# Attention scores from queries and keys split into a rounded part and a rest

## What is computed

```python
def _L1_xattn_ref(x, context, Wq, Wk, Wv, Wo, bo):
    HEADS, DIM_HEAD = 16, 64
    SCALE = DIM_HEAD ** (-0.5)
    q = (x @ Wq).reshape(B, N, HEADS, DIM_HEAD).transpose(0, 2, 1, 3)
    k = (context @ Wk).reshape(B, M, HEADS, DIM_HEAD).transpose(0, 2, 1, 3)
    v = (context @ Wv).reshape(B, M, HEADS, DIM_HEAD).transpose(0, 2, 1, 3)
    dots = jnp.einsum('bhnd,bhmd->bhnm', q, k) * SCALE
    attn = jax.nn.softmax(dots, axis=-1)
    out = jnp.einsum('bhnm,bhmd->bhnd', attn, v)
    out = out.transpose(0, 2, 1, 3).reshape(B, N, HEADS * DIM_HEAD)
    return out @ Wo + bo
# L2 is the same with HEADS = 8
x = x + _L1_xattn_ref(_layernorm(x, axis=-1), ctx_768, ...)
...
x = x + _L2_xattn_ref(_layernorm(x, axis=-1), ctx_768, ...)
```

## Time and profile before

| | |
|---|---|
| median of 3 runs | 1681.1 us (1678.39 to 1681.11) |
| the profiled execution | 1681.9 us |
| its span, first to last instruction | 1679.2 us |
| l1x, first to last scores matmul | 342.2 to 705.3 us |
| l2x, first to last scores matmul | 829.6 to 1026.5 us |
| busy over the whole span | PE 86%, DVE 59%, ACT 47%, POOL 36% |

### The profile page before, as it was taken

One profiled execution on the slowest core, in us unless ns is written; L12 is line 12 of the kernel. 1 busy time (PEld: TensorE's weight loads), 2 busy tenths in 40 slices (PEclk: granted clock), 3 DMA queues, 4 the chain that ended last, 5 costly groups with the idle time before them and its releaser, 6 DMA issues. The chain is left out here.

```text
span 1679.2 us, 28447 instructions
## 1 busy us (share of the span) xinstructions
PE 1436.1 (86%) x9255; PEld 1137.2 (68%) x9255; DVE 985.6 (59%) x2396; ACT 793.9 (47%) x1920; POOL 604.3 (36%) x807
## 2 busy tenths in 40 slices
PE   4698999699999999959699997884877569999995
PEld 3477888577777777735477675463544459989885
DVE  3768888855555555559666655445775624334342
ACT  2543444465555555448665654432757333333331
POOL 0137999463343443330264442000102622222222
PEclk9789999899999999989799999897888679999998
DMA  8000023319500000010000001005003821111110
GB/s 279 20 13 20 23 98 112 99 57 291 143 2 1 2 2 1 1 38 1 16 1 1 2 1 56 20 1 220 36 1 101 281 80 52 47 52 48 53 45 6
DMA packets 67340, 97.47 MB, mean 58 GB/s; under 512 B 7792, under 2 KB 56832, under 8 KB 66176
## 3 DMA queue, kind: packets, MB, share of 16 engines
q1 hardware_dynamic: 61920, 82.94, 15.8%
q0 software_dynamic: 5280, 12.74, 2.3%
HBM read 61.86 MB, written 35.63 MB: 58 GB/s over the span
## 5 line engine op out<-in xcount | busy, mean ns | idle before, releaser
L1325 POOL TENSOR_SCALAR XT<-XT,l1x_rs 128x256 f32<-128x256 f32 x256 | 117.7, 478 | 191.5 <-DVE l1x_rs L1209 191.5
L2502 PE MATMUL bank<-l3x_wd,CT 128*128 x624 | 146.4, 389 | 9.2 <-issue 8.7
L1213 DVE TENSOR_REDUCE l1x_nmax<-bank 128x2 f32<-128x512 f32 x128 | 87.4, 684 | 109.9 <-PE bank L1035 109.9
L1152 ACT ACTIVATE XT<-bank,l1x_nmax 128x256 f32<-128x256 f32 x256 | 118.8, 471 | 68.5 <-DVE l1x_nmax L1213 68.5
L2490 PEld LDWEIGHTS bank<-XT,l3x_qw 128*128 128x128 f32 x1248 | 148.0, 195 | 3.5 <-issue 0.9
L2490 PE MATMUL bank<-XT,l3x_qw 128*128 128x128 f32 x1248 | 148.4, 278 | 1.0 <-issue 0.5
L2502 PEld LDWEIGHTS bank<-l3x_wd,CT 128*128 128x128 f32 x624 | 117.8, 194 | 28.6 <-issue 13.3
L1047 PE MATMUL bank<-ident,XT 128*128 128x128 f32 x768 | 120.7, 280 | 7.5 <-DVE l2x_pt L1220 3.5
L759 DVE SCALAR_TENSOR_TENSOR X<-bank,l0f_gates,X 128x256 f32<-128x256 f32 x288 | 118.9, 473 | 0.7 <-PE bank L683 0.7
L1047 PEld LDWEIGHTS bank<-ident,XT 128*128 128x128 f32 x768 | 84.6, 140 | 41.3 <-issue 20.7
L1220 DVE COPY l1x_pt<-bank 128x512 f32<-128x512 f32 x128 | 87.8, 686 | 30.8 <-PE bank L1047 30.8
(11 more groups left out here) (526 smaller groups left out, 3887.3 us busy)
## 6 DMA issues: line engine op xcount, KB each, us to landing
slots<-blank SPq DMA_DIRECT2D x9, 1987.5 KB, 22.2
l3x_wu<-in_L_ffn_W SPq DMA_DIRECT2D x8, 1024.0 KB
l3x_wd<-in_L_ffn_W SPq DMA_DIRECT2D x8, 1024.0 KB
XT<-slots SPq DMA_DIRECT2D x39, 132.5 KB, 2.1
l0f_wu<-in_L_ffn_upT SPq DMA_DIRECT2D x18, 128.0 KB, 2.2
l0f_wd<-in_L_ffn_downT SPq DMA_DIRECT2D x18, 128.0 KB, 2.4
X<-in_x SPq DMA_DIRECT2D x1, 2048.0 KB, 8.2
l0x_later<-in_L_xattn_W_f1T SPq DMA_DIRECT2D x1, 2048.0 KB
```

Of the source, the lines that this page charges most:

```text
L1152: act.activation(pr[n % 3][:, i, q, :], sc[(2 * n + i) % 3][:, q * S:(q + 1) * S], ACT.Exp, bias=nmax[:, n % 3, i, q:q + 1], accum_out=sum ...
L1213: dve.tensor_reduce(nmax[:, n % 3, i, :], sc[(2 * n + i) % 3][:].rearrange("p (q s) -> p q s", q=QT), AX, ALU.max, negate=True).then_inc(m ...
L1325: pool.tensor_scalar(t, t, rs[:, n % 3, i, q:q + 1], 1.0, ALU.mult, ALU.mult).then_inc(norm_ok, 1)
L2502: last = pe.matmul(y_b[i % 2][:, 0:D], hT[i % 2][:, m, :], wd[:, ds(e * HT + m, 1), :].rearrange("p a n -> p (a n)"), start=m == 0, stop=m ...
```

## The change

The tile `qk` becomes two float32r tiles. ACT writes the rounded part `qk_hi` from the PSUM bank, and a new DVE operation, `low_qk`, subtracts it from the same bank into `qk_lo`. The scores become three products into the same PSUM region, hi x hi, hi x lo and lo x hi, with the two heads alternating inside each term. Three waits are added: `scores(n)` waits for `qklo_ok`, a unit that follows a qk unit in its bank waits for `qklo_ok` too, and `low_qk` waits for ACT's copy of its unit and for the earlier scores on its buffer. `low_qk` stands in DVE's queue between the maximum of head 1 and the copy of head 1. `LEAD` is 4.

```diff
@@ -902,7 +902,7 @@
         xn = [flat[:, 3072 + s * 512:3584 + s * 512].rearrange("p (t d) -> p t d", t=QT) for s in range(2)]
         xhi, xlo = ([sb(f"{n}{s}", [P, KD, S], F32R) for s in range(2)] for n in ("xhi", "xlo"))
         chi, clo = ([sb(f"{n}{s}", [P, kt, S], F32R) for s in range(2)] for n, kt in (("chi", 2), ("clo", 1)))
-        qk = [sb(f"qk{s}", [P, 2, S]) for s in range(LEAD)]
+        qk_hi, qk_lo = ([sb(f"qk{n}{s}", [P, 2, S], F32R) for s in range(LEAD)] for n in ("hi", "lo"))
         v = [sb(f"v{s}", [P, 2, CH]) for s in range(2)]
         pt = [sb(f"pt{s}", [P, 2, 2 * S]) for s in range(2)]
         ohi, olo = ([sb(f"{n}{s}", [P, 2, S], F32R) for s in range(2)] for n in ("ohi", "olo"))
@@ -910,8 +910,8 @@
 
         w_hi, wqk_lo, wv_lo, wo_lo, w_zero, bo_ok, split_done = (
             K.sem(f"{name}_{x}") for x in ("whi", "wqklo", "wvlo", "wolo", "wzero", "bo", "split"))
-        xn_ok, xlo_ok, c_hi, c_ok, unit_done, unit_read = (
-            K.sem(f"{name}_{x}") for x in ("xn", "xlo", "chi", "c", "unitdone", "unitread"))
+        xn_ok, xlo_ok, qklo_ok, c_hi, c_ok, unit_done, unit_read = (
+            K.sem(f"{name}_{x}") for x in ("xn", "xlo", "qklo", "chi", "c", "unitdone", "unitread"))
         s_done = [K.sem(f"{name}_sdone{i}") for i in range(2)]
         pv_done = [K.sem(f"{name}_pvdone{i}") for i in range(2)]
         max_done, exp_done, rs_ok, norm_ok, t_done, pt_ok = (
@@ -979,6 +979,8 @@
                         pe.wait_ge(unit_read, number[before[u]] + 1)
                         if before[u][0] == "x":
                             pe.wait_ge(xlo_ok, before[u][1] + 1)
+                        if before[u][0] == "qk":
+                            pe.wait_ge(qklo_ok, before[u][1] + 1)
                     if kind == "x":
                         pe.wait_ge(xn_ok, QT * (m + 1))
                         for k in range(KD):
@@ -1029,13 +1031,16 @@
                     pe.wait_ge(unit_read, number["qk", n] + 1)
                     if 4 * n - 2 > 0:
                         pe.wait_ge(exp_done, 4 * n - 2)
+                    pe.wait_ge(qklo_ok, n + 1)
+                    hi, lo = qk_hi[n % LEAD], qk_lo[n % LEAD]
                     for q in range(QT):
-                        for i in range(2):
-                            r = slice(i * DH, (i + 1) * DH)
-                            last = pe.matmul(sc[(2 * n + i) % 3][:, q * S:(q + 1) * S], qk[n % LEAD][r, 0, q * P:(q + 1) * P],
-                                             qk[n % LEAD][r, 1, :], start=True, stop=True)
-                            if q == QT - 1:
-                                last.then_inc(s_done[i], 1)
+                        for term, (x, y) in enumerate(((hi, hi), (hi, lo), (lo, hi))):
+                            for i in range(2):
+                                r = slice(i * DH, (i + 1) * DH)
+                                last = pe.matmul(sc[(2 * n + i) % 3][:, q * S:(q + 1) * S], x[r, 0, q * P:(q + 1) * P], y[r, 1, :],
+                                                 start=term == 0, stop=term == 2)
+                                if q == QT - 1 and term == 2:
+                                    last.then_inc(s_done[i], 1)
 
                 def turn(n, i):
                     pe.wait_ge(norm_ok, 2 * QT * n + QT * (i + 1))
@@ -1114,7 +1119,7 @@
                         if m >= LEAD:
                             for i in range(2):
                                 act.wait_ge(s_done[i], m - LEAD + 1)
-                        act.activation(qk[m % LEAD][:], t, ACT.Copy).then_inc(unit_read, 1)
+                        act.activation(qk_hi[m % LEAD][:], t, ACT.Copy).then_inc(unit_read, 1)
                     elif kind == "m":
                         act.activation(view.row[0:1, m, :], place[u][0:1, 0:P], ACT.Copy).then_inc(unit_read, 1)
                     elif kind == "s":
@@ -1204,6 +1209,14 @@
                     dve.tensor_tensor(xlo[b % 2][:], place["x", b][:].rearrange("p (a s) -> p a s", a=2), xhi[b % 2][:].bitcast(F32),
                                       ALU.subtract).then_inc(xlo_ok, 1)
 
+                def low_qk(m):
+                    dve.wait_ge(unit_read, number["qk", m] + 1)
+                    if m >= LEAD:
+                        for i in range(2):
+                            dve.wait_ge(s_done[i], m - LEAD + 1)
+                    dve.tensor_tensor(qk_lo[m % LEAD][:], place["qk", m][:].rearrange("p (a s) -> p a s", a=2), qk_hi[m % LEAD][:].bitcast(F32),
+                                      ALU.subtract).then_inc(qklo_ok, 1)
+
                 def inverse(n):
                     dve.wait_ge(exp_done, 4 * (n + 1))
                     dve.reciprocal(rs[:, n % 3, :, :], sums[:, n % 3, :, :]).then_inc(rs_ok, 1)
@@ -1276,6 +1289,8 @@
                 for k in range(2):
                     dve.wait_ge(w_hi, 4 + k + 1)
                     lo_part(raw_v, wv, k, wv_lo, rows=HALF_C if k else P)
+                low_qk(0)
+                low_qk(1)
                 for n in steps[1:]:
                     if (n - 3) % HP == 0 and 1 <= (n - 3) // HP < B:
                         add((n - 3) // HP - 1)
@@ -1290,6 +1305,8 @@
                         copy_turned(n, 0)
                     if 0 <= n + 2 < N:
                         maximum(n + 2, 1)
+                    for kind, m in first[n]:
+                        low_qk(m)
                     if view and n >= 1:
                         look(n - 1)
                     if 0 <= n < N:
```

## The result

The changed kernel takes 1685.5 us at the median against 1679.4 us for the kernel before on the same chip: ratio 1.0033, 95% interval 1.0022 to 1.0043. A repeat on another occasion gave 1.0052 (1.0035 to 1.0068), and is among the experiments. So it is slower, by a third to half of a per cent. The forecast was about 1682 us, 0.8 us more than before, with a chance of 0.35 for slower. The measured median lies inside the range of 1672 to 1698 us, but the change costs about 6 us and not 0.8.

The account below looks back on a forecast made before the run. The prediction took PE's queue to bound both stages. Shorter scores and added waits summed to -15.4 + 4.9 + 11.3 = +0.8 us, taking the profiled 1681.9 to 1682.7 us and the median to about 1682; range 1672 to 1698 us.

Parts of the forecast that it names:

- The scores: Scores of each step: six slots of 0.12 us, 0.91 us instead of 1.07, 15.4 us less over 96 steps.
- Rival 1: Scores: the slot is 0.11 us, 21 us saved and 16.2 lost, 1676 us; chance 0.18.
- rivals 4 and 5: Scores: heads' loads take turns, 42 us more, chance 0.07; or heads don't run side by side, 54 us more, chance 0.03.
- The chain from the copy to the next unit: Unit behind a qk unit: must wait for ACT's copy and DVE's subtraction, 1.47 us from the copy's start.
- l1x: Stage with 64 scores: 10.2 us gained in the scores, 4.9 us lost to waits.
- The plain odd steps: l1x, 23 steps: PE waits 0.12 us before the projection of values, 2.8 us in all.
- The seven odd steps behind a turned x: l1x, where a batch is added: the unit starts later, 0.3 us each, 2.1 us in all.
- l2x: Stage with 32 scores: 5.1 us gained in the scores, 11.3 us lost to waits, mostly at side units.
- The four odd steps with values alone: l2x: waits at the projection of values, 0.7 us in all.
- Rival 2: Waits cost less than counted, since late units eat slack: sum -8 us, 1673 us; chance 0.13.
- Rival 3: DVE's queue stays late, so turn(n, 1) waits for head 0's copy: 14 us, 1696 us; chance 0.21.
- The upper bound of 0.143 us a slot: Scores: if load and matmul add up, a step costs 1.05 us and 2 us are saved.

Follow-up runs that it names:

- e9: The changed kernel without the second and third score term of head 1; ratio to the kernel before 1.0024 (1.0005 to 1.0043).
- e4: The changed kernel, but ACT copies queries and keys whole to SBUF, freeing the bank, and DVE makes both parts there; ratio to the kernel before 0.9934.
- e7: The changed kernel with each subtraction done twice and the bank released behind the second; ratio to the kernel before 1.0344.
- e11: The changed kernel without the product of the queries' rest with the rounded keys, both subtractions kept; ratio to the kernel before 0.9932.
- e10: The changed kernel with all six score matmuls of head 0 ahead of all six of head 1; ratio to the kernel before 1.0212.
- e6: The changed kernel with three score matmuls of head 0 ahead of three of head 1 in each query tile; ratio to the kernel before 1.0059.

## Why the prediction was nearly right, and what it missed

**The scores.** Right to the hundredth: 0.91 us, slots of 0.12 us in pairs, from the float32r projections as nearest row. Rival 1 (slot 0.11) falls, as do rivals 4 and 5 (1.51 and 1.63 us), the latter two by e9 as well.

**ACT's copy and the subtraction.** 0.60 and 0.69 us as predicted, hidden as busy time. The chain from the copy to the next unit was put at 1.47 us and took 1.42.

**l1x.** Predicted 5.3 us shorter, measured 6.7 us. The term that was too large is the wait: 3.5 us instead of 4.9, and place by place it was further off than that. The plain odd steps gave back some 0.02 us each, 0.5 us in all, and not 0.12 us each, 2.8 us: the chain is 0.05 us shorter than the sum of its parts, and most of what is left is made up behind it. The seven odd steps behind a turned x gave back 0.23 us each, 1.6 us against 2.1. The other 1.4 us were not in the sum. 0.8 us of them is the wait for the copy for head 1 at 356.66, of which the prediction said that its delay costs nothing; that holds in the middle of the stage and not at its start. So the sum for l1x is better than its parts deserve.

**l2x.** Predicted 6.2 us longer, measured 11.7. This is the step that failed, and it has two parts. The waits that PE shows came to 11.8 us against 11.3, right in sum but not place by place, which is partly luck. The steps 9 and 17 gave 0.77 each as said; 5 and 15 gave 2.4 us instead of 2.6; 0 and 1 gave 1.8 instead of 0.8; 7, 11, 19, 23 and 27 gave 4.5 instead of 5.7; the steps 4, 22 and 26, which my list left out, gave 1.5. The four odd steps with values alone were put at 0.7 us; they show no idle time and lost 0.4 us. The other part was missing altogether: PE's busy time should have dropped by 5.1 us and did not drop. Two falls of the clock, some 3 us, are seen; I had computed idle times of 1.5 us and more and never asked what they would do to the clock. The last 2 us, the 0.4 us among them, are located but not explained. In e4, with neither these waits nor the falls, the 5 us are there.

**Rival 2** (waits cost less) holds in l1x by 1.4 us and is wrong in l2x. **Rival 3** (the copy of head 0 late) did not occur: DVE still idles 1.2 to 1.8 us before the maximum in ordinary steps of l1x.

**Two readings that were wrong.** The upper bound of 0.143 us a slot came from 64 matmuls between 97.87 and 107.02 us of the kernel before. The granted clock was 1.00 up to 102.80 (47 matmuls in flight in 4.93 us, about 0.11 us each) and 0.50 behind that (22 in 4.22 us, about 0.19 each), so the bound mixes the two levels. And the side units of l2x were to show "about 1.5 us idle"; the prediction's own 0.25 + 0.77 gives 1.02, which is what the plain ones show.

**Range and chances.** The measured 0.33% equals 5.6 us on the profiled 1681.9, past the 3.4 us that I had called distinguishable. Against the +5.0 us of the stages the sum of +0.8 us is 4.2 us short: 5.5 us are missing in l2x, and 1.4 us too many in l1x hide part of it. The time lies in the range partly by luck, for the upper end stood for rival 3 and for the bound of the slot, and neither is what made the kernel slower. The chances don't follow from each other as written: 0.38 less 0.3 of it leaves 0.27 for "same", not 0.34, and about 0.40 for slower.

## What to carry to other kernels

Splitting an operand into two parts on the way out of PSUM costs little as work and much as a held bank: look for who needs that bank next, and copy it out whole first if the split can be made from SBUF. That turned a loss of 0.3 to 0.5% into a gain of 0.7%. When a sum contains idle times of TensorE of the size seen here, 1.6 us and more, add a term for its clock, and compare stages by their own lengths when the rest of the program scatters by more than the effect.

## What the runs showed of the hardware beyond expectation

- In l2x, TensorE at the full clock fell to the 1.2 GHz level at single idle times of 1.63 to 2.58 us, for 3 to 4 us (once, in e7, for 7), at about 1.5 us of lost time for a short fall. It did so twice in the changed kernel, three times in e11 and five times in e7. It did not at eight idle times of 1.74 to 1.77 us in e7, nor at 1.67, 1.85 and 1.88 us in e10. What else decides is open.
- Matmuls of two heads on different rows share a slot even with three others between them in the program (e6, 0.91 us), and only partly with six (e10, 1.25 us).
- DVE operations with all operands in SBUF took from 0.42 up to 1.58 us (cast) and from 0.69 up to 1.68 us (subtraction) in e4's l2x. At the two slow rows shown above GpSimd was at work on SBUF tensors from 854.36 to 858.16 without much of a break, and the subtraction from a PSUM bank took 0.69 us in all 96 cases of the changed kernel. The Trainium skill (SBUF — State Buffer, SBUF: two separate sides) describes a port pair of the two engines that one holds for a whole instruction; the rows agree with that, and no run here took GpSimd away to show it.
